# Search rounds of a top-k: one threshold count moved from VectorE's accumulator and ScalarE's signs to TensorE passes over masks

## What is computed

```python
input_acts = gelu(jnp.einsum('bsd,nd->bsn', x, input_patterns))      # 2048 per token
input_acts_seq = input_acts.mean(axis=1)                             # 64 x 2048
top_input_acts, top_input_idx = jax.lax.top_k(input_acts_seq, 256)
input_repr = zeros.at[brow, top_input_idx].set(top_input_acts)
process_acts = gelu(jnp.einsum('bn,pn->bp', input_repr, process_input_weights))   # 64 x 1024
top_process_acts, top_process_idx = jax.lax.top_k(process_acts, 128)
aggregated_value = softmax(top_process_acts) @ process_values[top_process_idx]
output_acts_seq = gelu(jnp.einsum('bd,od->bo', aggregated_value, output_input_weights))  # 64 x 2048
top_output_acts, top_output_idx = jax.lax.top_k(output_acts_seq, 256)
out_per_seq = jnp.einsum('bk,bkm->bm', top_output_acts, output_patterns[top_output_idx])
output = broadcast(out_per_seq) + residual
```

## Time and profile before

| what | value |
|---|---|
| median of 3 runs | 1633.43 us |
| the profiled execution | 1632.56 us |
| its span in the trace | 1630.8 us |
| busy in the span: TensorE passes / loads, VectorE, ScalarE | 1461.4 / 1369.6, 971.0, 940.4 us |
| `route` in the span | from about 1400 us to the end |

### The profile page before, as it was taken

One profiled execution on the slowest core, in us unless ns is written; L12 is line 12 of the kernel. 1 busy time (PEld: TensorE's weight loads), 2 busy tenths in 40 slices (PEclk: granted clock), 3 DMA queues, 4 the chain that ended last, 5 costly groups with the idle time before them and its releaser, 6 DMA issues. The chain is left out here.

```text
span 1630.8 us, 31726 instructions
## 1 busy us (share of the span) xinstructions
PE 1461.4 (90%) x9685; PEld 1369.6 (84%) x9685; DVE 971.0 (60%) x2429; ACT 940.4 (58%) x3348; POOL 116.8 (7%) x243
## 2 busy tenths in 40 slices
PE   5899999999999999999999999999999998764321
PEld 4799999999999999999999999999999998661220
DVE  6766655555555555555555555555565543585686
ACT  4566666666666666666666666666666654761440
POOL 0000000000000000000000000000000000000000
PEclk9999999999999999999999999999999999757555
DMA  9311111111111111111111111111110000376007
GB/s 202 81 45 45 45 44 44 44 41 41 40 43 44 44 44 44 44 44 44 44 42 40 39 40 39 40 40 40 40 40 10 10 11 11 105 245 263 0 0 315
DMA packets 53092, 99.35 MB, mean 61 GB/s; under 512 B 16704, under 2 KB 35648, under 8 KB 52032
## 3 DMA queue, kind: packets, MB, share of 16 engines
q1 hardware_dynamic: 50768, 96.91, 20.4%
q10 hardware_dynamic: 2288, 2.00, 0.6%
HBM read 73.17 MB, written 25.69 MB: 61 GB/s over the span
## 5 line engine op out<-in xcount | busy, mean ns | idle before, releaser
L625 ACT ACTIVATE ffn<-ffn 128x196 f32<-128x196 f32 x1024 | 329.0, 321 | 208.4 <-PE ffn L513 207.9
L513 PE MATMUL ffn<-x_t_hi,pat_w_hi 128*128 128x392 f32 x1024 | 361.7, 353 | 1.7 <-DVE x_t_lo L780 1.7
L513 PE MATMUL ffn<-x_t_lo,pat_w_hi 128*128 128x392 f32 x1024 | 348.5, 340 | 0.0
L513 PE MATMUL ffn<-x_t_hi,pat_w_lo 128*128 128x392 f32 x1024 | 348.4, 340 | 0.0
L716 DVE SCALAR_TENSOR_TENSOR shared<-shared,gen 98x512 f32<-98x512 f32 x64 | 44.0, 688 | 278.4 <-ACT shared L598 278.4
L513 PEld LDWEIGHTS ffn<-x_t_hi,pat_w_hi 128*128 128x128 f32 x1024 | 192.9, 188 | 6.1 <-DVE x_t_lo L780 2.0
L513 PEld LDWEIGHTS ffn<-x_t_lo,pat_w_hi 128*128 128x128 f32 x1024 | 194.3, 190 | 1.2
L625 ACT ACTIVATION_READ_ACCUMULATOR ffn<-ffn 128x1 f32 x1024 | 193.1, 189 | 0.0
L513 PEld LDWEIGHTS ffn<-x_t_hi,pat_w_lo 128*128 128x128 f32 x1024 | 193.0, 189 | 0.0
L443 PE MATMUL gen<-qkvu_w_hi,h_t_hi 128*98 128x512 f32 (+1 forms) x512 | 172.4, 337 | 2.4 <-ACT q_t L580 2.1
L443 PE MATMUL gen<-qkvu_w_lo,h_t_hi 128*98 128x512 f32 (+1 forms) x512 | 172.5, 337 | 0.0
(11 more groups left out here) (209 smaller groups left out, 2743.1 us busy)
## 6 DMA issues: line engine op xcount, KB each, us to landing
raw<-in_x_dram SPq DMA_DIRECT2D x752, 56.0 KB, 2.0
h_dram<-h SPq DMA_DIRECT2D x128, 98.0 KB
process_nat<-ocess_input_weights_dram SPq DMA_DIRECT2D x8, 1024.0 KB, 4.8
process_t<-h_dram SPq DMA_DIRECT2D x8, 896.0 KB, 12.0
out_dram<-process_t SPq DMA_DIRECT2D x8, 896.0 KB, 6.7
h_early<-h_dram SPq DMA_DIRECT2D x4, 896.0 KB, 12.7
out_dram<-h_early SPq DMA_DIRECT2D x4, 896.0 KB, 4.0
pat_nat<-_ffn_input_patterns_dram SPq DMA_DIRECT2D x1, 2048.0 KB, 15.8
```

Of the source, the lines that this page charges most:

```text
L513: last = pe.matmul(fb[f % FFN_BANKS][:, 0:T2], a[:, d, f * P:(f + 1) * P], b[:, d, :], start=n == 0, stop=n == 3 * s.halves - 1)
L625: last = act.activation(cols, cols, ACT.Gelu, accum_out=gelu_sum[:, par, at:at + 1])
```

## The change

Two of the three counts no longer come from accumulators. VectorE writes masks of ones and zeros (bf16), with no accumulator: for the first threshold all 1024 values, in two halves of 512; for the second all 1024; for the third the last 256 (`SHARED_AT` is now 3/4 of 1024). Each mask adds one to a new semaphore `masked`. ScalarE takes signs for the third threshold alone, over the first 768 values. TensorE folds each mask: it multiplies blocks of 64 columns by `image_sum` (now bf16) and adds all blocks of one threshold into the same 64 columns of PSUM, 36 products a round, and adds the signs by one product of 4 columns into the third group. VectorE then adds up the 64 columns of each group with a new reduction of 3 x 64 out of PSUM, and a further wait stands ahead of the comparison with 256. There is one PSUM tile for the tallies in place of two. The constant product is gone: the constant now stands in a second column of `signs`, which `blank` fills once. `search_steps` gives the third threshold twice (for VectorE, and half a step lower for ScalarE) in place of the second.

```diff
-        SHARED_AT = 5 * HALF // 8
-        reached_too = sb("reached_too", [P, 2 * HALF - SHARED_AT], BF16)
+        SHARED_AT, BLOCK = 3 * HALF // 4, 64
+        reached_too = sb("reached_too", [P, HALF], BF16)
+        reached.append(reached_too[:])
+        masked_parts = [[slice(0, HALF // 2), slice(HALF // 2, HALF)], [slice(0, HALF)], [slice(SHARED_AT, HALF)]]
+        MASKS = sum(map(len, masked_parts))
...
-        blank = sb("blank", [P, 12])
-        numbers = sb("numbers", [P, 12], F32R)
-        count, signs, offset = (numbers[:, n:n + 4] for n in (0, 4, 8))
-        image_sum = sb("image_sum", [P, P], F32R)
+        blank = sb("blank", [P, 4])
+        signs = sb("signs", [P, 4], F32R)
+        counts = sb("counts", [P, 3])
+        image_sum = sb("image_sum", [P, P], BF16)
...
-            pool.memset(blank[:, 9:10], (HALF - SHARED_AT) / 2)
-            pool.memset(blank[:, 10:11], HALF / 2).then_inc(masks_made, 1)
+            pool.memset(blank[:, 1:2], float(-SHARED_AT)).then_inc(masks_made, 1)
...
             def sum_halves(n):
-                tally = tallies[n % 2][:, 0:4]
                 if n == 0:
                     pe.wait_ge(numbers_made, 1)
-                if n >= 2:
-                    pe.wait_ge(judged, n - 1)
-                pe.matmul(tally, image_sum[:], offset, start=True, stop=False)
+                for m, parts in enumerate(masked_parts):
+                    for part, cols in enumerate(parts):
+                        pe.wait_ge(masked, MASKS * n + sum(map(len, masked_parts[:m])) + part + 1)
+                        for at in range(cols.start, cols.stop, BLOCK):
+                            pe.matmul(tally[:, m * BLOCK:(m + 1) * BLOCK], image_sum[:], reached[m][:, at:at + BLOCK],
+                                      start=at == parts[0].start, stop=at == HALF - BLOCK and m < 2)
                 pe.wait_ge(counted_too, n + 1)
-                pe.matmul(tally, image_minus_half[:], signs, start=False, stop=False)
-                pe.wait_ge(counted, n + 1)
-                pe.matmul(tally, image_sum[:], count, start=False, stop=True).then_inc(summed, 1)
+                pe.matmul(tally[:, 2 * BLOCK:2 * BLOCK + 4], image_minus_half[:], signs[:],
+                          start=False, stop=True).then_inc(summed, 1)
...
-                    act.activation(reached_too[:, 0:HALF], word[:], ACT.Sign, scale=-1.0, bias=tried[:, 4:5],
-                                   accum_out=signs[:, 2:3])
-                    act.activation(reached_too[:, HALF:], word[:, SHARED_AT:], ACT.Sign, scale=-1.0,
-                                   bias=tried[:, 3:4], accum_out=signs[:, 1:2]).then_inc(counted_too, 1)
+                    act.activation(reached_too[:, 0:SHARED_AT], word[:, 0:SHARED_AT], ACT.Sign, scale=-1.0,
+                                   bias=tried[:, 4:5], accum_out=signs[:, 0:1]).then_inc(counted_too, 1)
...
-                        for m, cols in enumerate((HALF, SHARED_AT)):
-                            last = dve.tensor_scalar(reached[m][:, 0:cols], word[:, 0:cols], tried[:, 1 + m:2 + m],
-                                                     0.0, ALU.is_ge, ALU.add, accum_out=count[:, m:m + 1])
-                        last.then_inc(counted, 1)
+                    for m, parts in enumerate(masked_parts):
+                        for cols in parts:
+                            dve.tensor_scalar(reached[m][:, cols], word[:, cols], tried[:, 1 + m:2 + m], None,
+                                              ALU.is_ge).then_inc(masked, 1)
...
                     dve.wait_ge(summed, n + 1)
-                    dve.tensor_scalar(passed[:], tallies[n % 2][:, 0:3], float(s.k_in), 0.0, ALU.is_ge, ALU.add,
+                    dve.reduce_sum(counts[:], tally[:, 0:3 * BLOCK].rearrange("p (m b) -> p m b", b=BLOCK),
+                                   axis=AX.X).then_inc(counted, 1)
+                    dve.wait_ge(counted, n + 1)
+                    dve.tensor_scalar(passed[:], counts[:], float(s.k_in), 0.0, ALU.is_ge, ALU.add,
                                       accum_out=found[:]).then_inc(judged, 1)
...
-    rounds = np.stack([0 * size, size, 2 * size, 2 * size - 0.5, 3 * size - 0.5, size], axis=1)
+    rounds = np.stack([0 * size, size, 2 * size, 3 * size, 3 * size - 0.5, size], axis=1)
```

More of the change, by code:

```diff
@@ L957, in route @@
         sums = ctx.enter_context(nc.psum_tensor("sums", [P, 512], F32))
-        tallies = [sums, turn[2]]
+        tally = turn[2]
         prod = [ctx.enter_context(nc.psum_tensor(f"rp{b}", [P, 512], F32)) for b in range(4)]
@@ L963, in route @@
         acts_turned, wide_made, chosen = sem("acts_turned"), sem("wide_made"), sem("chosen")
-        words_made, tried_made, numbers_made, counted, counted_too = sem("words_made"), sem("tried_made"), sem("numbers_made"), sem("counted"), sem("counted_too")
+        words_made, tried_made, numbers_made, counted, counted_too, masked = sem("words_made"), sem("tried_made"), sem("numbers_made"), sem("counted"), sem("counted_too"), sem("masked")
         summed, ahead_made, judged = sem("summed"), sem("ahead_made"), sem("judged")
@@ L1184, in _ @@
             act.activation(image_minus_half[:], same_image[:], ACT.Copy, scale=-0.5)
-            act.activation(numbers[:], blank[:], ACT.Copy).then_inc(numbers_made, 1)
+            act.activation(signs[:], blank[:], ACT.Copy).then_inc(numbers_made, 1)
             act.activation(both_halves[:], same_image[:, 0:B].unsqueeze(2).to_broadcast([P, B, 2]), ACT.Copy)
@@ L1244, in try_three @@
                     n, at = search * ROUNDS + r, 6 * r
-                    if n == 0:
-                        dve.wait_ge(numbers_made, 1)
-                    with nc.allow_low_precision(reason="whole numbers up to 1024"):
-                        for m, cols in enumerate((HALF, SHARED_AT)):
-                            last = dve.tensor_scalar(reached[m][:, 0:cols], word[:, 0:cols], tried[:, 1 + m:2 + m],
-                                                     0.0, ALU.is_ge, ALU.add, accum_out=count[:, m:m + 1])
-                        last.then_inc(counted, 1)
+                    for m, parts in enumerate(masked_parts):
+                        for cols in parts:
+                            dve.tensor_scalar(reached[m][:, cols], word[:, cols], tried[:, 1 + m:2 + m], None,
+                                              ALU.is_ge).then_inc(masked, 1)
                     dve.tensor_scalar(ahead[:], steps[:, at + 6:at + 11], tried[:, 0:1], None,
```

## The result

| | before | changed |
|---|---|---|
| median of 16 runs each, us | 1633.85 (1632.18 to 1636.79) | 1643.44 (1637.47 to 1645.67) |
| ratio to before, 95% interval | | 1.0050 (1.0042 to 1.0059) |
| the profiled execution, us | 1632.56 | 1643.92 |
| its span; mean granted TensorE clock | 1630.8; 0.937 | 1642.2; 0.946 |
| busy VectorE, ScalarE, us | 971.0, 940.4 | 953.8, 916.0 |

A forecast was written before the change was run, and what follows sets the result against it. The prediction took the search rounds' sign counts, ScalarE and VectorE side by side, 32 rounds on the path, as the bound. First top-k -0.2 and last +7.7 gave 1633.43 + 7.5 = 1641 us, range 1627 to 1656.

The forecast's parts named there:

- Masks: VectorE's masks at a round's start: 0.49, 0.36 and 0.30 us for 1024, 512 and 256 elements, ending at 1.27.
- Rival 3: VectorE's masks take 0.754 us per 1024 elements, rounds 3.93 slow and 3.53 fast: 1655 us, chance 0.09.
- Signs: ScalarE's 768 signs a round: 0.93 us, 1.03 with the accumulator read, covered by the passes.
- Passes at 1.2 GHz: TensorE's 64-column passes over the masks at the low clock: 0.053 us each, 1.91 for 36.
- Rival 2: Every TensorE pass waits for its own load of 128 columns: 1654 us, or 1682 with the last top-k slow; chance 0.14.
- Passes at 2.4 GHz: TensorE's 64-column passes over the masks at the high clock: 0.037 us each.
- Last product to sums: From a round's last TensorE product to its sums: 0.33 us at the low clock, 0.25 at the high.
- Rounds: A search round: 3.57 us at 1.2 GHz, 0.48 more than before; 3.01 at 2.4 GHz, 0.08 less.
- Clock: TensorE's clock: 2 slow and 14 fast rounds in the first top-k, 16 slow in the last.
- Rivals 1 and 4: First: clock high in both top-k, 1627 to 1634 us, chance 0.36. Fourth: clock never rises, 1650 us, chance 0.07.
- Queue: First top-k's transposes between rounds on TensorE: at the low clock until 4.0 us, next mask at 3.99, just fits.
- Sum: Both top-k together: -0.2 us in the first, +7.7 in the last, +7.5 in all.

The follow-up runs named there:

- f2: The changed kernel with blocks of 32 columns in place of 64, 72 passes a round: 1647.47 us, ratio 1.0075 to the kernel before.
- f3: The changed kernel with blocks of 128 columns in place of 64, 18 passes a round: 1647.84 us, ratio 1.0083 to the kernel before.
- e1: The changed kernel with idle products on TensorE behind each round of the last top-k, 13 or 40 of them: 1632.83 us, ratio 0.9987 to before.
- e3: The changed kernel with 48 idle products once, ahead of the first round of the last top-k: 1643.9 us, ratio 1.0051 to before.
- g3: The kernel before with 11 idle transposes behind each round of the last top-k, 28 between its searches: 1634.11 us, ratio 0.9999 to before.
- e4: The changed kernel without VectorE's mask of the third threshold, ScalarE counting all of it, 32 passes a round: 1640.5 us, ratio 1.0029 to before.
- e2: The changed kernel with idle f32 transposes behind each round of the last top-k, 8 or 24 of them: 1629.33 us, ratio 0.9973 to before.
- f1: The changed kernel with both e2's idle transposes (28 between searches) and e4's dropped mask: 1630.78 us, ratio 0.9974 to before.

## Why the prediction was right

The forecast was 1641 us and slower; the median is 1643.44. Step by step:

- **Masks**: 0.49, 0.36 and 0.30 were taken as the middle between two ends; the groups by shape in the last top-k show 0.480, 0.350 and 0.280:

```profile
L1248 DVE TENSOR_SCALAR chosen_t<-word,tried 128x512 bf16<-128x512 int16 x32 | 9.8, 350 | 0.6
L1248 DVE TENSOR_SCALAR chosen_t<-word,tried 128x1024 bf16<-128x1024 int16 x16 | 7.7, 480 | 0.0
L1253 DVE TENSOR_REDUCE counts<-rt 128x3 f32<-128x192 f32 x16 | 5.7, 357 | 21.9 <-PE rt L1071 21.9
L1248 DVE TENSOR_SCALAR reached_too<-word,tried 128x256 bf16<-128x256 int16 x16 | 4.5, 280 | 0.0
```

  Rival 3 is out. TensorE starts 0.41 after the round's start (0.42 forecast). The reduction takes 0.357 (0.35) and the tail 1536.86 - 1535.94 = 0.92 (0.91).
- **Signs**: 0.94 and the accumulator until 1.03 (1534.26 - 1533.23), as forecast and covered.
- **Passes at 1.2 GHz**: 0.053, as taken from L499. Rival 2 (each pass waits for its load) is out: f2 and f3.
- **Passes at 2.4 GHz**: mis-sized. L499's row gave 0.037. The last four of the round above take (1421.57 - 1421.45)/4 = 0.030, which was the lower end, L457's pace. In a round the last product starts 1.66 after the start instead of 1.85, 0.04 of it because the second mask ends at 1.01 and not at 1.05.
- **Last product to sums**: mis-sized the other way, 1535.94 - 1535.55 = 0.39 against 0.33, and 1421.86 - 1421.57 = 0.29 against 0.25.
- **Rounds**: 3.63 instead of 3.57 (+0.06 for the last product and 0.01 for the tail, less 0.01); 2.87 instead of 3.01 (-0.19 + 0.04 + 0.01).
- **Clock**: the step that decides, and right: high in the first top-k but for its start (the first distance is 3.32) and the second round behind the pause (3.69), where the forecast had two slow rounds, both at the start, low in all 16 rounds of the last. e1 and e3 show that it is this, and that the loop's pauses, left empty, keep it low. Rivals 1 and 4 are out. But the stretch that the forecast read this from was a narrow witness: with 8 transposes a round the clock stayed at 0.50 there, with 11 in g3 it rose and fell; and rival 1, which lost here, had been given 0.36 against the forecast's 0.34.
- **Queue**: "just fits" was a little off. At the low clock the transposes of the first top-k hold TensorE until 0.64 after the next round's start (1411.49 - 1410.85) and, behind the pause, until 0.60 after it (1437.85 - 1437.25), where 0.42 was forecast. That is some 0.2 us in each of two rounds.
- **Sum**: -0.2 for the first top-k became -1.4, +7.7 for the last became +8.7. That 7.3 came out for the forecast 7.5 is luck: two terms were off by 1 us, one each way. The ratio's interval is worth 6.9 to 9.6 us. What the medians show beyond 7.5, 2.1 us, is about the size of the 2.2 us that the stretch between the two top-k lost in the profiled execution, which the prediction didn't consider; that it is the same isn't shown.

## What to carry to other kernels

Before work is moved to TensorE, price the loop at both levels of its clock and ask what TensorE does in the rest of the loop: the same edit gave 0.22 us a round where transposes followed the passes and took 0.54 where nothing did. Where a loop leaves pauses on TensorE, idle work in them can be worth more than a shorter loop (e1: some 10 us, e4: 2.9), and a warm-up ahead of the loop alone gained nothing (e3). Small passes should be priced with a floor: at the high clock halving the columns saved one sixth of a pass (0.030 to 0.025) and doubled their number.

## What was not expected of the hardware

- Idle f32 transposes lift the clock and hold it with rounds of passes between them (e2, f1: 0.96 to 1.00 but for the start); nearly alone they lift it and don't hold it (g3, 11 a round); in the first top-k before, real ones, 8 a round, left it at 0.50.
- A TensorE pass of 32 columns takes 0.027 us at the low clock and 0.025 at the high one; at the low clock the same weights loaded again ahead of each pass cost nothing in these rows, at 128, 64 or 32 columns.
- The granted clock differs between executions of one kernel, and the time with it: among the 16 runs of the changed kernel from 1637.47 us at a mean of 0.951 to 1645.67 at 0.945. A profile shows one execution; a step of 2 us can't be read from two profiles.
